# A language-model tower on one core: the normalised attention input scaled on ScalarE, its product in another PSUM bank, and two reorderings

## The reference

```python
normed = (xf - mu) / jnp.sqrt(var + 1e-05) * ln_g + ln_b
x_attn = normed @ attn_w.T + attn_b + xf          # xf = layernorm(h)
tok = x_attn.reshape(MICRO_BATCHES, e, t, d)
h1 = gelu(einsum('meti,ehi->meth', tok, fc1_w) + fc1_b)
y  = einsum('meth,edh->metd', h1, fc2_w) + fc2_b
out = gelu(y @ next_w.T + next_b)                 # and h + out is returned
```

## Time and profile before

| | us |
|---|---|
| median of 3 runs | 188.5 |
| profiled execution, its own time | 188.72 |
| its span | 186.9 |
| PE busy | 169.2 (91%) |
| DVE busy | 135.4 (72%) |
| ACT busy | 108.6 (58%) |
| POOL busy | 106.5 (57%) |
| granted TensorE clock, mean | 0.997 |

### The profile page before, as it was taken

One profiled execution on the slowest core, in us unless ns is written; L12 is line 12 of the kernel. 1 busy time (PEld: TensorE's weight loads), 2 busy tenths in 40 slices (PEclk: granted clock), 3 DMA queues, 4 the chain that ended last, 5 costly groups with the idle time before them and its releaser, 6 DMA issues.

```text
span 186.9 us, 3886 instructions
## 1 busy us (share of the span) xinstructions
PE 169.2 (91%) x1327; PEld 154.3 (83%) x1327; DVE 135.4 (72%) x410; ACT 108.6 (58%) x289; POOL 106.5 (57%) x173
## 2 busy tenths in 40 slices
PE   0598899999999999799898899999999999997993
PEld 0187779999989999688587899999999999986882
DVE  1868974775444446667988999988889898628883
ACT  3026997745443334543445496785949778595782
POOL 3107664699900000323979678397896969789600
PEclk9999999999999999999999999999999999999998
DMA  5994000000000000000000000001010100101003
GB/s 147 321 438 182 5 0 5 2 0 0 4 0 0 4 0 0 2 4 0 0 0 0 4 0 2 4 2 56 0 60 0 53 7 2 58 4 58 24 32 112
DMA packets 2327, 7.42 MB, mean 40 GB/s; under 512 B 254, under 2 KB 892, under 8 KB 2052
## 3 DMA queue, kind: packets, MB, share of 16 engines
q1 hardware_dynamic: 2162, 7.05, 10.0%
q10 hardware_dynamic: 146, 0.13, 0.2%
HBM read 5.09 MB, written 2.10 MB: 38 GB/s over the span
## 4 chain that ended last, share of the span: by engine, by line
PE 53%; POOL 14%; DVE 12%; issue 9%; ACT 8%; DMA 2%; ACTq 0%; POOLq 0%; DVEq 0%
PE bank L966 8%; PE bank L969 7%; PE bank L1106 6%; POOL hid_p L437 6%; PE bank L1126 5%; PE bank L994 5%; PE bank L1053 4%; POOL rstd L467 3%; PE bank L943 3%; PE bank L899 2%; PE bank L920 2%; PE bank L983 2%; PE bank L1050 2%; ACT gel L560 2%; POOL X L449 2%
## 5 line engine op out<-in xcount | busy, mean ns | idle before, releaser
L437 POOL TENSOR_TENSOR hid_p<-hid_f,hid_p 128x256 fp32r<-128x256 f32 x52 | 37.5, 741 | 14.5 <-ACT hid_p L602 12.6
L600 ACT ACTIVATE hid_f<-bank,pa 128x256 f32<-128x256 f32 x64 | 30.8, 485 | 12.7 <-PE bank L1106 12.5
L1106 PE MATMUL bank<-xaT_p,fc_p 128*128 128x256 f32 x192 | 35.4, 296 | 1.7 <-ACT corr L577 0.7
L1126 PE MATMUL bank<-hid_p,out_hi 128*128 128x256 f32 x128 | 32.0, 286 | 0.3 <-POOL hid_p L437 0.3
L509 ACT ACTIVATE X<-bank 128x128 f32<-128x128 f32 x64 | 17.6, 278 | 22.7 <-PE bank L969 22.5
L1106 PEld LDWEIGHTS bank<-xaT_p,fc_p 128*128 128x128 f32 x192 | 26.7, 189 | 4.7 <-ACT hid_p L602 1.7
L966 PE MATMUL bank<-uT,pa 128*128 128x128 f32 x128 | 25.2, 281 | 0.1
L1126 PEld LDWEIGHTS bank<-hid_p,out_hi 128*128 128x128 f32 x128 | 23.3, 188 | 1.0 <-POOL hid_p L437 0.6
L602 ACT ACTIVATE hid_p<-bank,pa 128x256 fp32r<-128x256 f32 x48 | 23.5, 489 | 0.0
L969 PE MATMUL bank<-X,pa 128*128 128x128 f32 x120 | 23.2, 275 | 0.0
L444 POOL TENSOR_TENSOR E<-E,corr 128x248 f32<-128x248 f32 (+4 forms) x5 | 3.1, 626 | 32.0 <-ACT corr L585 32.0
(11 more groups left out here) (126 smaller groups left out, 369.8 us busy)
## 6 DMA issues: line engine op xcount, KB each, us to landing
fc_w<-in_fc SPq DMA_DIRECT2D x2, 2048.0 KB, 12.1
out<-res SPq DMA_DIRECT2D x7, 256.0 KB, 2.0
pb<-in_pack_b SPq DMA_DIRECT2D x1, 320.0 KB, 4.1
pa<-in_pack_a SPq DMA_DIRECT2D x1, 279.0 KB, 3.0
out<-res SPq DMA_DIRECT2D x2, 128.0 KB, 1.7
pc<-in_pack_c ACTq DMA_DIRECT2D x1, 128.5 KB, 3.0
pw<-in_pack_a SPq DMA_DIRECT2D x1, 64.0 KB, 3.8
emb_w<-in_emb SPq DMA_DIRECT2D x1, 62.5 KB
```

The costliest lines, as they stand in the source:

```text
L437: nc.gpsimd.tensor_tensor(hid_p[1][:, half, c, :], hid_f[:, m % HID_SLOTS, :], hid_p[0][:, half, c, :].bitcast(F32), ALU.subtract).then_in ...
L600: full = nc.scalar.activation(hid_f[:, m % HID_SLOTS, :], src, ACT.Gelu, bias=bias)
L1106: last = mm(bank[5 + n % 2][:, 0:HALF], fc1_p[w][:, e * HID + c * P:e * HID + (c + 1) * P], xaT_p[m][:, b % 2, half, :], start=(k == 0), s ...
L1126: last = mm(out_bank(b, half)[:, half * HALF:(half + 1) * HALF], out_p[w][:, e, c * CH:(c + 1) * CH], hid_p[m][:, half, c, :], start=(c == ...
```

## The change

Four edits. VectorE's L782 goes; ScalarE computes xa from the bank by four activations with a scale and a bias pointer, in place 0 of its round, behind the gelus of piece 0. For this the bias must be minus mean x rstd0: VectorE writes minus the mean as a third small value into `spread2`, and Pool multiplies that by rstd0, last of its group, with a semaphore of its own. The attention product goes into bank 3, where `transpose_xa` writes as well, so `attn` waits until the low part of xaT has been read; `transpose_h` waits for the hT copy of the sequence before instead of xa. VectorE's low part of xaT moves behind the statistics and spread of the next sequence. Pool's power, ratio and shift move ahead of the subtraction and the scan's adds of place 3.

```diff
-        spread2 = sb("spread2", [P, 2, 2, NQ])
+        spread2 = sb("spread2", [P, 2, 3, NQ])
+        shift2_ready = sem("shift2_ready")
 # Pool: at the start of the loop body, ahead of the subtraction and the scan's adds
+                        b = j + 2
+                        if n == 3 and 0 <= b < NB:
+                            pool.wait_ge(v2_ready, b + 1)
+                            nc.gpsimd.tensor_tensor(rstd2[:, b, :, :]..., spread2[:, b % 2, 0:2, :]..., neg_half[:],
+                                                    ALU.pow).then_inc(rstd2_ready, 1)
+                            pool.wait_ge(rstd2_ready, b + 1)
+                            if b >= 2:
+                                pool.wait_ge(xa_ready, b - 1)
+                            chained(nc.gpsimd.tensor_tensor(part[:, 1, :], spread2[:, b % 2, 1, :], r1, ALU.mult))
+                            nc.gpsimd.tensor_tensor(part[:, 0, :], part[:, 1, :], r0, ALU.mult).then_inc(ratio2_ready, 1)
+                            nc.gpsimd.tensor_tensor(shift2[:, b % 2], spread2[:, b % 2, 2, :], r0,
+                                                    ALU.mult).then_inc(shift2_ready, 1)
 # ScalarE: behind the gelus of place n, ahead of the xaT copy of place 1
+                        if n == 0 and 0 <= b < NB:
+                            act.wait_ge(shift2_ready, b + 1)
+                            act.wait_ge(xs_ready, b + 1)
+                            if b >= 1:
+                                act.wait_ge(xa_t_done, b)
+                            for q in range(NQ):
+                                s = slice(q * CH, (q + 1) * CH)
+                                last = nc.scalar.activation(xa[:, s], bank[3][:, s], ACT.Identity,
+                                                            scale=rstd2[:, b, 1, q:q + 1], bias=shift2[:, b % 2, q:q + 1])
+                            last.then_inc(xa_ready, 1)
 # VectorE: sequence j + 1
-                                out=bank[4][:, s], in0=h[:, b, s], scalar=ratio2[:, b % 2, 0, q:q + 1],
-                                in1=bank[4][:, s], op0=ALU.mult, op1=ALU.add)
+                                out=bank[3][:, s], in0=h[:, b, s], scalar=ratio2[:, b % 2, 0, q:q + 1],
+                                in1=bank[3][:, s], op0=ALU.mult, op1=ALU.add)
                         last.then_inc(xs_ready, 1)
-                        dve.wait_ge(xs_ready, b + 1)
-                        for q in range(NQ):
-                            s = slice(q * CH, (q + 1) * CH)
-                            last = nc.vector.tensor_scalar(xa[:, s], bank[4][:, s], rstd2[:, b, 1, q:q + 1],
-                                                           shift2[:, b % 2, q:q + 1], ALU.mult, ALU.subtract)
-                        last.then_inc(xa_ready, 1)
 # VectorE: h, statistics and spread of sequence j + 2 now stand ahead of the low part of xaT of j + 1; new in it:
+                            dve.wait_ge(shift2_ready, b - 1)
+                        nc.vector.tensor_scalar(t[:, 2, :], mv2[:, b, :, 0], -1.0, None, ALU.mult)
 # TensorE
 def transpose_h(b):
-                        pe.wait_ge(xa_ready, b)
+                        pe.wait_ge(hT_ready, b)
 def attn(b):
                     pe.wait_ge(hT_ready, b + 1)
+                    if b == 0:
+                        pe.wait_ge(uT_ready, NB)
+                    else:
+                        pe.wait_ge(xaT_lo_ready, b)
-                        last = mm(bank[4][:, s], hT[:, b % HT_SLOTS, s], attn_m[:], start=True, stop=True)
+                        last = mm(bank[3][:, s], hT[:, b % HT_SLOTS, s], attn_m[:], start=True, stop=True)
```

More of the change, by code:

```diff
@@ L430, in _ @@
                     for n in range(8):
+                        b = j + 2
+                        if n == 3 and 0 <= b < NB:
+                            pool.wait_ge(v2_ready, b + 1)
+                            nc.gpsimd.tensor_tensor(rstd2[:, b, :, :].rearrange("p s q -> p (s q)"),
+                                                    spread2[:, b % 2, 0:2, :].rearrange("p s q -> p (s q)"), neg_half[:],
+                                                    ALU.pow).then_inc(rstd2_ready, 1)
+                            pool.wait_ge(rstd2_ready, b + 1)
+                            if b >= 2:
+                                pool.wait_ge(xa_ready, b - 1)
+                            r0, r1, part = rstd2[:, b, 0, :], rstd2[:, b, 1, :], ratio2[:, b % 2]
+                            chained(nc.gpsimd.tensor_tensor(part[:, 1, :], spread2[:, b % 2, 1, :], r1, ALU.mult))
+                            nc.gpsimd.tensor_tensor(part[:, 0, :], part[:, 1, :], r0, ALU.mult).then_inc(ratio2_ready, 1)
+                            nc.gpsimd.tensor_tensor(shift2[:, b % 2], spread2[:, b % 2, 2, :], r0,
+                                                    ALU.mult).then_inc(shift2_ready, 1)
                         if 0 <= j < DVE_ROUND or (DVE_ROUND <= j < NB - 1 and n % 2 == 0):
@@ L462, in _ @@
                                 ALU.add).then_inc(res_ready, 1)
[L463 to L477, removed]
             @block.scalar
@@ L799, in _ @@
                     high_parts(j, range(0, 2))
+                    b = j + 2
+                    if 0 <= b < NB:
+                        dve.wait_ge(y_done, b + 1)
+                        nc.vector.tensor_tensor(h[:, b, :], h[:, b, :], bank[2][:], ALU.add).then_inc(h2_ready, 1)
+                        dve.wait_ge(h2_ready, b + 1)
+                        statistics(b, st2, st2_ready, mv2, mv2_ready)
+                        if b >= 2:
+                            dve.wait_ge(shift2_ready, b - 1)
+                        dve.wait_ge(mv2_ready, b + 1)
+                        v, t = mv2[:, b, :, 1], spread2[:, b % 2]
+                        nc.vector.tensor_scalar(t[:, 2, :], mv2[:, b, :, 0], -1.0, None, ALU.mult)
+                        nc.vector.tensor_scalar(t[:, 0, :], v, EPS, None, ALU.add)
+                        nc.vector.tensor_scalar(t[:, 1, :], v, 1.0 + EPS, EPS * EPS, ALU.mult,
+                                                ALU.add).then_inc(v2_ready, 1)
                     b = j + 1
@@ L814, in _ @@
                         last.then_inc(xaT_lo_ready, 1)
[L815 to L828, removed]
                     if j < 0:
```

## The result

The changed kernel takes 190.49 us (median of four runs, 190.12 to 191.19) against 188.47 for the kernel before. The quotient of these medians is 1.0107; the ratio on record is 1.0118, with a 95% interval of 1.0099 to 1.0138, so the slowdown is clear of noise. Forecast were 190.4 us, and a span of 188.8; the profiled execution has a span of 188.7 and a time of 190.45.

The account below looks back on a forecast made before the run. TensorE, busy 91%, bounds the kernel: its own work and waits for gelus hold middle rounds at 10.98 us. Terms of 1.21, 0.34, 0.54 and 0.1, less 0.3, gave +1.9: 190.6, or 190.4 as median; range 188.5 to 192.0.

Parts of the forecast that it names:

- The front: Round -1: two scan adds wait behind Pool's power group, delaying the corr copy and the loop's first fc1 by 1.10 us.
- The strip: ScalarE's four xa activations behind part 0's gelus: 1.57 us, xa ready at 2.97 against TensorE's 2.83, costing 0.14 each middle round.
- The threshold of 1.42: ScalarE's xa activations in the middle rounds: if the four took under 1.42 us, their price would be zero.
- Two nearly equal paths: Middle rounds: ScalarE's path of 11.12 us and VectorE's cycle of 11.08 us are nearly equal.
- Pool's ratio: Ratio ahead of part 3's subtraction: saves VectorE's 0.44 us wait before the product, but gains nothing in the middle rounds.
- The sum: Whole span: +1.21 in round 0, +0.34 next, +0.54 over four more, +0.1 last, some 0.3 regained; total +1.9 us.
- the gain at the end: Round 6: Pool running some 0.4 us ahead takes a wait of 0.3 us out.
- The short strip: Rival: ScalarE's four xa activations take under 1.42 us, so xa is ready before TensorE arrives; 187.7 us, chance 0.11.
- a cheap front: Round -1's Pool delay at its lower bound, +0.2 us; with xa's activations short, 187.3 us.
- The second rival: ScalarE's xa activations take 1.43 us, Pool's delay is near its lower bound, gains cancel costs; 188.5 us, chance 0.11.
- The third rival: VectorE's small instructions stand behind a Pool subtraction, breaking margins of 0.35 and 0.4; cycle 11.5 to 11.6, 192.4 us, chance 0.15.

Follow-up runs that it names:

- e6: Kernel before with only Pool's power, shift and ratio moved ahead of place 3's subtraction and the scan's adds, in all rounds; 188.18 us (ratio 0.9984).
- e2: Changed kernel with xa computed on VectorE behind the product again, not by ScalarE's four activations; 188.79 us (ratio 1.0018).
- e1: Changed kernel with the scan's adds ahead of Pool's power, ratio and shift again in rounds -3 to -1 only; 190.15 us (ratio 1.0095).
- e3: Changed kernel with VectorE's low part of xaT ahead of h and the statistics again; 190.86 us (ratio 1.0121).
- e4: Changed kernel with ScalarE's four xa activations moved ahead of the gelus of part 0; 189.79 us (ratio 1.0072).
- e9: Changed kernel with two xa activations of 256 columns instead of four of 128, omitting groups 1 and 3's own scale and bias; 188.56 us (ratio 1.0020).
- e10: Changed kernel with a fifth activation of 128 columns ahead of ScalarE's four for xa; 193.24 us (ratio 1.0263).

## Why the prediction was right

- **The front.** Priced at +1.10 on the first fc1, measured 1.04; power predicted at 98.5, came at 98.38; e6 shows 0.87 of it alone. That it becomes a delay of xa of the same size (+1.10 at 105.75) needs the strip as well, as the prediction's sum has it: fc1, gelus, strip. In e2 and e6, without the strip, a first fc1 0.67 and 0.87 late leaves the transposes 0.06 early and 0.13 late. What the step did not see is the second margin in round -1, `attn` against the low part: it was worked out for the later rounds only (0.35 left) and for round 0 (0.3, measured wait 0.18). It is hidden in the changed kernel by 0.1 (the low part ends at 98.22 + 0.86, `attn` starts at 99.22), and in e1 it takes 0.6 of what the undone Pool move would give back.
- **The strip.** Taken as 1.57 between 1.43 and 1.65, measured 1.51: 0.465 each, a new one every 0.35. xa ready at 2.97 in the round, measured 2.93 (161.39 - 158.46). The mechanism is the predicted one: with a strip of 1.0 the cost is gone, at 1.51 it is 0.16 a round, at 1.85 it is 0.50. That 0.14 was forecast and 0.16 came is in part luck. In the round from 150.24, readiness alone makes 2.93 - 2.83 = 0.10. Another 0.07 lies behind the transposes, from their start to the next round's first fc1: 158.46 - 150.24 = 8.22, against 156.54 - 148.39 = 8.15 before, most of it in the transposes themselves (0.66 for 0.60). The prediction has no such term, and took the strip 0.06 too long instead. The threshold of 1.42 was not measured: it lies between 1.0 and 1.51.
- **Two nearly equal paths.** 11.12 and 11.08 predicted, 11.14 measured; e3 and e4 put ScalarE's at 11.14 and VectorE's at 11.08. VectorE's wait ahead of h is 2.5 us a round (2.4 predicted).
- **Pool's ratio.** By the rows it gains nothing in the changed kernel's middle rounds: the product starts at 158.56 with no wait ahead of it, behind xh on VectorE. No run undoes the move there alone. In the kernel before the same move takes 0.03 off each middle distance, and 0.8 off the last.
- **The sum.** +1.9 on the span, measured +1.8: the terms 1.21, 0.34, 0.54 and 0.1 came out as 1.10, 0.34, 0.58 and 0.12; the gain at the end is 0.4 instead of 0.3.
- **Rivals.** The short strip was made by hand (1.02 us) and gave 188.56, not 187.7. With the full price of the front the prediction put its first transposes at 105.24, and they came at 105.23; but it went on to +0.45 and then -0.3 at the end, where +0.58 and +0.1 came, and its 187.7 lay between that sum (188.2) and one with a cheap front. The second rival needed a strip of 1.43 and a front near +0.2; they were 1.51 and +1.04. The third rival's mechanism (VectorE's small instructions held up, the low part late) did not show in the middle rounds but did in e1's round -1.

## What to carry to other kernels

Moving work to a less busy engine pays only if the piece is ready before its consumer arrives: read the consumer's arrival and the new engine's queue ahead of the piece, and compare the two; the share of busy time says nothing here (58% for ScalarE, and still 0.16 us too late a round). When a small step that one engine waits for is moved to an early place, the rounds of another kind must be checked too, here round -1, where the adds behind it are waited for as well. The price of a late instruction depends on what follows it: the same late fc1 cost about 1 us at xa with the strip behind its gelus, and 0.2 to 0.4 with xa on VectorE. When an undone edit gives back a third of its price, look for a second wait stacked on the same instruction before doubting the first.

## What the runs showed of the hardware

- An activation of 128x128 from PSUM with scale and bias pointers takes 465 ns, the next one 0.35 us behind (changed kernel); of 128x256, 565 (e9). From SBUF the same form took 490 at 27.19. The Trainium skill, page "ScalarE: Activation LUTs", section "What ACT_TABLE_LOAD costs", gives 479 ns and 0.386 us; for PSUM the measured numbers decide, 1.51 for four instead of 1.64.
- The four transposes of xa take 0.60 us when xa is there before TensorE arrives (e9, 126.95; kernel before, 148.39) and 0.65 or 0.66 when TensorE waits for it (changed kernel, every round of the loop; e10).
- VectorE's instructions of 128x4 take 0.16 us, but 0.69 when Pool's adds run at the same time (e1, 98.24, four adds from 96.82 on, 2.76 for all); in the changed kernel, where Pool stands idle at that moment, the same instruction takes 0.15. It ends at 98.93, as Pool passes from one add to the next (96.82 + 3 x 0.69 = 98.89). The Trainium skill, page "SBUF — State Buffer", section "🔬 SBUF: two separate sides", says that the two engines share a port pair: of a GpSimd instruction and a VectorE instruction that runs in a two-port mode or has two SBUF inputs, the one that starts first holds the pair for its whole length, and the other waits. These rows agree in their times; whether the 128x4 instructions run in a two-port mode no row shows.
